# Column sums from the combined weight blocks T4 and T3 of a Strassen-Winograd kernel, with three sums of weight blocks made by accumulating transfers

## The reference

```
h = gelu(cond @ W0 + b0);  h = gelu(h @ W1 + b1)
att = softmax(h @ W2 + b2)                        # 128 samples x 8 kernels
agg_w = sum_k att[b,k] * weight[k]                # one 64x64 channel mix per sample
agg_b = att @ bias_k                              # one bias per sample and channel
y = agg_w[b] @ x[b] + agg_b[b][:, None]           # 128 x 64 x 1024
logits = y @ W_router.T;  top 2 of 8 experts, softmax weights
h = y @ A.T (8 experts x rank 16), weighted by expert
out = x + y @ W_base.T + b_base + (h weighted) @ B * 2.0
```

## Time and profile before

| | us |
|---|---|
| median of 3 runs | 951.85 (951.58 to 951.88) |
| profiled execution, its own time | 951.36 |
| its span, first to last instruction | 949.7 |
| TensorE busy | 942.1 |
| VectorE busy | 786.1 |
| ScalarE busy | 330.0 |
| GpSimd busy | 87.7 |

### The profile page before, as it was taken

The page is one execution under the profiler, slowest core; times in us unless marked ns, Lnnn a source line. Parts: engine busy times, 40 slices in busy tenths (PEclk is TensorE's granted clock), DMA queues, the critical chain, the costliest instruction groups (busy, mean ns, idle before and its releaser), DMA issues.

```text
span 949.7 us, 19258 instructions
## 1 busy us (share of the span) xinstructions
PE 942.1 (99%) x6716; PEld 935.7 (99%) x6716; DVE 786.1 (83%) x2018; ACT 330.0 (35%) x671; POOL 87.7 (9%) x134
## 2 busy tenths in 40 slices
PE   9999999999999999999999999999999999999998
PEld 8999999999999999999999999999999999999997
DVE  4999888888888888888888888888888888888886
ACT  6553332333332333333333333333332333323331
POOL 0011010101010100100000101010101010101010
PEclk9999999999999999999999999999999999999999
DMA  8443444343435344434344434344444444443434
GB/s 303 143 112 96 110 119 132 92 133 91 112 113 134 91 119 107 112 113 125 100 108 119 112 113 111 114 97 129 107 119 104 121 91 121 114 125 99 126 91 111
DMA packets 35234, 111.34 MB, mean 117 GB/s; under 512 B 13040, under 2 KB 13424, under 8 KB 30864
## 3 DMA queue, kind: packets, MB, share of 16 engines
q1 hardware_dynamic: 25712, 76.36, 22.1%
q0 software_dynamic: 9216, 33.56, 21.3%
q10 hardware_dynamic: 288, 1.19, 0.4%
HBM read 75.37 MB, written 35.65 MB: 117 GB/s over the span
## 4 chain that ended last, share of the span: by engine, by line
PE 95%; DVE 2%; DMA 1%; issue 1%; ACT 0%; DVEq 0%; ACTq 0%
PE ps L420 25%; PE ps L424 24%; PE ps L422 24%; PE ps L480 9%; PE ps L456 3%; PE ps L454 3%; PE ps L458 3%; DMA w_stage<-in_wide 1%; PE ps L503 1%; PE ps L446 0%; PE ps L447 0%; DVE x_sb L1025 0%; DMA result<-x_sb 0%; DVE lower_hwT L1007 0%; PE ps L506 0%
## 5 line engine op out<-in xcount | busy, mean ns | idle before, releaser
L420 PE MATMUL ps<-w_hi,x_hi 128*128 128x290 f32 x1544 | 461.0, 299 | 0.9 <-DVE z_lo L960 0.6
L422 PE MATMUL ps<-w_lo,x_hi 128*128 128x290 f32 x1544 | 458.4, 297 | 0.0
L424 PE MATMUL ps<-w_hi,x_lo 128*128 128x290 f32 x1544 | 457.5, 296 | 0.0
L420 PEld LDWEIGHTS ps<-w_hi,x_hi 128*128 128x128 f32 x1544 | 292.4, 189 | 3.5 <-issue 2.6
L424 PEld LDWEIGHTS ps<-w_hi,x_lo 128*128 128x128 f32 x1544 | 291.8, 189 | 0.0
L422 PEld LDWEIGHTS ps<-w_lo,x_hi 128*128 128x128 f32 x1544 | 291.7, 189 | 0.0
L689 ACT CAST x_hi<-xT_sb 128x512 fp32r<-128x512 f32 x186 | 115.6, 621 | 188.7 <-DVE xT_sb L943 166.4
L927 DVE TENSOR_TENSOR x_lo<-xT_sb,x_hi 128x512 fp32r<-128x512 f32 x186 | 127.1, 684 | 22.7 <-ACT x_hi L689 22.7
L904 POOL DMA_DIRECT2D x_sb<-in_x x64 | 56.3, 880 | 534.1 <-DVE x_sb L1025 534.1
L1007 DVE STREAM_TRANSPOSE lower_hwT<-hw 32x32 f32<-32x32 f32 x464 | 93.9, 202 | 13.6
L711 ACT COPY sum<-ps 128x580 f32<-128x580 f32 x96 | 61.6, 641 | 88.1 <-PE ps L424 88.1
(11 more groups left out here) (126 smaller groups left out, 1135.4 us busy)
## 6 DMA issues: line engine op xcount, KB each, us to landing
x_sb<-in_x POOLq DMA_DIRECT2D x64, 512.0 KB, 5.4
result<-x_sb SPq DMA_DIRECT2D x63, 512.0 KB, 2.8
xT_sb<-in_xT SPq DMA_DIRECT2D x31, 1024.0 KB, 4.8
b_sb<-in_wide SPq DMA_DIRECT2D x2, 1160.0 KB, 14.4
agg_w_rows<-agg_w SPq DMA_DIRECT2D x1, 2048.0 KB, 7.5
mix<-agg_w_rows SPq DMA_DIRECT2D x124, 16.0 KB, 3.1
w_stage<-in_wide ACTq DMA_DIRECT2D x2, 580.0 KB, 7.4
w_stage<-in_wide SPq DMA_DIRECT2D x2, 580.0 KB, 10.9
```

Source lines behind the costliest of these rows:

```text
L420: nc.tensor.matmul(dst, x_hi[:, s, rows], high[:, c, cols], start=first, stop=False, skip_group_check=True)
L422: nc.tensor.matmul(dst, x_hi[:, s, rows], low[:, c, cols], start=False, stop=False, skip_group_check=True)
L424: mm = nc.tensor.matmul(dst, x_lo[:, s, rows], high[:, c, cols], start=False, stop=last, skip_group_check=True)
```

## The change

The T's get other signs and another way of being made. T3 is now B12 + B22, T4 is (B21 + B11) - T3, T1 = B12 - B11 as before, T2 = B22 + T1. The signs of S1, S2 and S3 follow. B21 + B11, T3 and T2 are made in place, in the stages of B21, B12 and B22, by accumulating transfers that GpSimd issues in halves (`add_block`): the first two read B11 and the next two B22 from DRAM again, the last two read T1 from the on-chip stage. VectorE makes T1 (now ahead of B22's low part) and T4 only. The column sums run over T4 and T3 in place of B11, B21, B12 and B22: those over T3 are the right half, and those over T4 and T3 together, added on VectorE, the left half. The products A21xB12 and A22xB22 come ahead of the column sums. The small result for agg_b goes to another bank, and ScalarE copies it out instead of VectorE. The low parts of T4, T3 and T2 are all made before unit 1, that of T1 within it, and tile 1's biases come later in unit 1.

```diff
--- before.py
+++ after.py
...
-B11, B21, T1, B22, T2, T4, T3 = range(7)
-B12 = T4
+
+B11, B21, T3, B22, T2, T4, T1 = range(7)
+B12 = T3
...
-        SPLIT_AT = {"B11": 4, "B21": 6, "B12": 7, "B22": 8, "T1": 9, "T2": 10, "T3": 11, "T4": 12}
+        SPLIT_AT = {"B11": 4, "B21": 6, "B12": 7, "B22": 8, "T4": 9, "T3": 10, "T2": 11, "T1": 12}
...
-        T_AT = {"T1": 1, "T2": 2, "T4": 3, "T3": 4}
+        T_AT = {"T1": 1, "T4": 2}
...
-        b11_stage = t_stage = chunked(w_stage[:, 0, :])
+
+        b11_stage = t1_stage = chunked(w_stage[:, 0, :])
         b2_stage = t4_stage = chunked(w_stage[:, 1, :])
-        b12_stage = chunked(b12_sb[:])
-        b22_stage = chunked(b22_sb[:])
+        b12_stage = t3_stage = chunked(b12_sb[:])
+        b22_stage = t2_stage = chunked(b22_sb[:])
...
-            def column_sums(bank, w, start=False, stop=False):
+            def column_sums(bank, w):
                 high, low = weight_parts(w)
                 for part in range(2):
                     dst, cols = ps[:, bank + part, 0:PART], slice(part * PART, (part + 1) * PART)
                     for c in range(CHUNKS):
-                        nc.tensor.matmul(dst, ones_r[:], high[:, c, cols], start=start and c == 0, stop=False)
-                        mm = nc.tensor.matmul(dst, ones_r[:], low[:, c, cols], start=False,
-                                              stop=stop and c == CHUNKS - 1)
-                if stop:
-                    mm.then_inc(col_mm, 1)
+                        nc.tensor.matmul(dst, ones_r[:], high[:, c, cols], start=c == 0, stop=False)
+                        mm = nc.tensor.matmul(dst, ones_r[:], low[:, c, cols], start=False, stop=c == CHUNKS - 1)
+                mm.then_inc(col_mm, 1)
 
...
@@ -568,29 +572,31 @@
             pe.wait_ge(w_lo_done, SPLIT_AT["B22"])
             first_product(b, "A12", B22, False)
             pe.wait_ge(agg_done, 2 * GROUPS)
-            chain(ps[:, O_BANK, 0:BATCH], mix_w_sb[0:KERNELS, GROUP_COLS:MIX_COLS], attT[0:KERNELS, :], agg_b_mm)
+            chain(ps[:, O_BANK + 3, 0:BATCH], mix_w_sb[0:KERNELS, GROUP_COLS:MIX_COLS], attT[0:KERNELS, :], agg_b_mm)
+            first_product(O_BANK, "A21", B12, True)
+            first_product(O_BANK, "A22", B22, False)
             pe.wait_ge(ones_done, 1)
-            column_sums(O_BANK + 2, B11, start=True)
-            column_sums(O_BANK + 2, B21, stop=True)
             pe.wait_ge(agg_b_done, 2)
-            first_product(O_BANK, "A21", B12, True)
-            pe.wait_ge(col_sum_done, 1)
-            column_sums(O_BANK + 2, B12, start=True)
-            first_product(O_BANK, "A22", B22, False)
-            column_sums(O_BANK + 2, B22, stop=True)
+            pe.wait_ge(w_lo_done, SPLIT_AT["T4"])
+            column_sums(O_BANK + 2, T4)
+            pe.wait_ge(z12_summed, 1)
+            pe.wait_ge(w_lo_done, SPLIT_AT["T3"])
+            column_sums(b, T3)
             pe.wait_ge(z22_summed, 1)
             pe.wait_ge(mix_lo_done, 1)
             pe.wait_ge(z11_lo_done, 1)
             mixed(0, 0).then_inc(ar_mm, 1)
             pe.wait_ge(z12_lo_done, 1)
             mixed(0, 1)
-            pe.wait_ge(col_sum_done, 2)
+            pe.wait_ge(col_sum_done, 1)
             mixed(0, 2).then_inc(mixed_mm, 1)
 
             def unit(u, par, first=False):
                 a, b = accumulators(par)
                 pe.wait_ge(z12_summed, u)
                 pe.wait_ge(x_lo_done, splits(u, "A11"))
+                if first:
+                    pe.wait_ge(col_sum_done, 2)
                 product(a, "A11", True)
...
+                if first:
+                    pe.wait_ge(w_lo_done, SPLIT_AT["T1"])
                 product(b, "S1", True)
...
-                if first:
-                    pe.wait_ge(w_lo_done, SPLIT_AT["T3"])
...
-                if first:
-                    pe.wait_ge(w_lo_done, SPLIT_AT["T4"])
...
-            def column_sum(half):
+            def column_sum(half, bank):
                 act.wait_ge(col_mm, half + 1)
                 cols = col_sum[:, half * HALF:(half + 1) * HALF].rearrange("p (k n) -> p k n", k=2)
-                nc.scalar.copy(cols, acc(O_BANK + 2)).then_inc(col_sum_done, 1)
+                nc.scalar.copy(cols, acc(bank)).then_inc(col_sum_done, 1)
...
@@ -787,23 +791,31 @@
             split_weight(B22, b22_stage)
             aggregated(0)
             z11_high(0)
+            act.wait_ge(xT_in, 16)
+            act.wait_ge(product_mm, FIRST_PRODUCT["A11", B12])
+            x_high("A11")
             aggregated(1)
-            act.wait_ge(t_made, T_AT["T1"])
-            split_weight(T1, t_stage)
             act.wait_ge(product_mm, FIRST_PRODUCT["A12", B22])
             save(sum2, b, z12_summed)
-            act.wait_ge(xT_in, 16)
-            x_high("A11")
-            column_sum(0)
+            act.wait_ge(agg_b_mm, 1)
+            for par in range(PAIR):
+                rows = slice(par * CH, (par + 1) * CH)
+                of_tiles = ps[rows, O_BANK + 3, 0:BATCH].rearrange("p (t par) -> p t par", par=PAIR)[:, :, par]
+                nc.scalar.copy(agg_b[rows, :], of_tiles).then_inc(agg_b_done, 1)
+            z12_high(0)
+            x_high("A12")
+            act.wait_ge(t_made, T_AT["T4"])
+            split_weight(T4, t4_stage)
+            act.wait_ge(product_mm, FIRST_PRODUCT["A21", B12])
+            split_weight(T3, t3_stage)
+            act.wait_ge(product_mm, FIRST_PRODUCT["A22", B22])
+            save(sum3, O_BANK, z22_summed)
             for side in range(2):
                 mix_high(0, side)
-            z12_high(0)
-            act.wait_ge(t_made, T_AT["T2"])
-            split_weight(T2, t_stage)
-            x_high("A12")
-            act.wait_ge(product_mm, FIRST_PRODUCT["A22", B22])
-            save(sum3, O_BANK, z22_summed)
-            column_sum(1)
+            act.wait_ge(t2_in, 32)
+            split_weight(T2, t2_stage)
+            column_sum(0, O_BANK + 2)
+            column_sum(1, b)
             act.wait_ge(bT_in, 16)
             nc.scalar.copy(b_hi[:], bT_stage).then_inc(b_hi_done, 1)
...
-                    act.wait_ge(t_made, T_AT["T3"])
-                    split_weight(T3, t_stage)
+                    act.wait_ge(w_lo_done, SPLIT_AT["T3"])
+                    split_weight(T1, t1_stage)
...
-                if first:
-                    split_weight(T4, t4_stage)
...
+            def add_block(dst, block, done):
+                for js in HALVES:
+                    cols = slice(js.start * HALF, js.stop * HALF)
+                    pool.dma_start(dst[:, cols], block[:, cols], accum_op=ALU.add).then_inc(done, 16)
+
+
+            pool.wait_ge(b22_in, 16)
+            pool.wait_ge(w_lo_done, SPLIT_AT["B21"])
+            add_block(w_stage[:, 1, :], wide_blocks[0], left_in)
+            pool.wait_ge(t_made, T_AT["T1"])
+            pool.wait_ge(w_lo_done, SPLIT_AT["B12"])
+            add_block(b12_sb[:], wide_blocks[3], t3_in)
+            pool.wait_ge(w_lo_done, SPLIT_AT["B22"])
+            add_block(b22_sb[:], w_stage[:, 0, :], t2_in)
...
             def make_s1(u):
-                nc.vector.tensor_tensor(raw("S1"), raw("A21"), raw("A22"), ALU.add).then_inc(s_made, 1)
+                nc.vector.tensor_tensor(raw("S1"), raw("A21"), raw("A22"), ALU.subtract).then_inc(s_made, 1)
...
-                nc.vector.tensor_tensor(raw("S3"), raw("A11"), raw("A21"), ALU.subtract).then_inc(s_made, 1)
+                nc.vector.tensor_tensor(raw("S3"), raw("A21"), raw("A11"), ALU.subtract).then_inc(s_made, 1)
...
-                nc.vector.tensor_tensor(raw("S2"), raw("S1"), raw("A11"), ALU.subtract).then_inc(s_made, 1)
+                nc.vector.tensor_tensor(raw("S2"), raw("A11"), raw("S1"), ALU.subtract).then_inc(s_made, 1)
...
             split_weight(B12, SPLIT_AT["B12"], b12_stage)
+            dve.wait_ge(w_lo_done, SPLIT_AT["B11"])
+            make_t(t1_stage, b12_stage, b11_stage)
             split_weight(B22, SPLIT_AT["B22"], b22_stage)
-            dve.wait_ge(w_lo_done, SPLIT_AT["B11"])
-            make_t(t_stage, b12_stage, b11_stage)
             z11_low(0)
             dve.wait_ge(xT_in, 16)
             make_s1(1)
             make_s3(1)
-            dve.wait_ge(agg_b_mm, 1)
-            for par in range(PAIR):
-                rows = slice(par * CH, (par + 1) * CH)
-                of_tiles = ps[rows, O_BANK, 0:BATCH].rearrange("p (t par) -> p t par", par=PAIR)[:, :, par]
-                nc.vector.tensor_copy(agg_b[rows, :], of_tiles).then_inc(agg_b_done, 1)
-            split_weight(T1, SPLIT_AT["T1"], t_stage)
             x_low(1, "A11")
-            dve.wait_ge(w_lo_done, SPLIT_AT["T1"])
-            dve.wait_ge(t_made, T_AT["T1"])
-            make_t(t_stage, b22_stage, t_stage)
+            dve.wait_ge(left_in, 32)
+            dve.wait_ge(t3_in, 32)
+            make_t(t4_stage, t4_stage, t3_stage)
             z12_low(0)
-            dve.wait_ge(t_made, T_AT["T2"])
-            make_t(t4_stage, b2_stage, t_stage)
```

(43 more changed lines are left out.)

## The result

The changed kernel takes 959.85 us (median of 6 runs, 959.19 to 960.6), the kernel before on the same chip 951.87 (951.5 to 952.32): a ratio of 1.0084 [1.0073, 1.0095], 8.0 us slower. The forecast was 956.5, slower with 0.82, with 953 to 959.5 for its main case and 951.8 to 961.5 for 8 in 10: the time lies 0.35 above the first and inside the second. The profiled execution took 960.6 with a span of 958.6, 8.9 over the span of before. The profile first, in the order in which the prediction asked for it.

The account below looks back on a forecast made before the run. The prediction took TensorE to bound the kernel, busy 942.1 of 949.7 us. Unit 1 4.9 later, +0.5 for late bT, -0.3 for unit 2's wait: +5.1 on 951.36 gives 956.5 us, range 951.8 to 961.5 for 8 in 10.

Parts of the forecast that it names:

- T: The moment the first four accumulating transfers have landed, so that VectorE can make T4; taken as 39.0 us.
- What bounds, and the 4.3 us of sums: TensorE bounds the kernel; before unit 1, 32 column-sum matmuls instead of 64 save 4.3 us if nothing it needs comes later.
- faster rival: Accumulating transfers run like plain ones, 1.6 us each, T about 31, unit 1 at 45.2: 946.8 us; chance 0.08.
- T = 39.0, by the mean's price: GpSimd's queue: first landing at 28.3, three more at 3.6 us each, the run's mean for adds of x scaled to 580 KB.
- the pair's price: 3.15 us per further 580 KB transfer, scaled from two adds of x issued one behind the other; would give T 37.8.
- All are queued long before their turn.: GpSimd's issues take 0.9 us each, so all six transfers are queued early and the queue's throughput sets T.
- T2 is needed at T+21.: T2's transfers land by T+7.2, its low part is ready about T+12.4 and needed at T+21.
- T to unit 1, 13.6 + 1.8: From T through T4's parts, the sums and mixing to unit 1: 13.6 us, plus 1.8 for TensorE's slow clock.
- slow stretch: TensorE's column sums and mixing at half clock after about 7 us idle: 0 to 5.9 us, taken as 1.8.
- Late bT, 0 to 1.4, taken 0.5: bT's load waits for agg_w's slowed copy, delaying b_hi and z21 in unit 1: 0 to 1.4 us, taken 0.5.
- the wait of unit 2, -0.3: TensorE's 0.6 us wait early in unit 2 may go as VectorE is 2.5 us lighter: 0 to 0.6, taken 0.3.
- later rival: The fourth transfer shares the engines with agg_w's copy, T = 44.8, unit 1 at 60.2, +10.4: 961.8 us; chance 0.10.

Follow-up runs that it names:

- e4_plain: The changed kernel with its six transfers as plain copies, without accumulation (the additions left out): 947.51 us, 0.9972 of the kernel before.
- e2: The changed kernel with descriptor room for GpSimd's transfers of 3072 instead of 1024: 957.99 us, 1.0072 of the kernel before.
- e3: e2 with 46 thrown-away matmuls while TensorE waits for T4's low part: 959.72 us, 1.0090 of the kernel before.
- g3: f1 with 28 thrown-away matmuls while TensorE waits for T4's low part: 952.42 us, 1.0008 of the kernel before.
- f3: f2 with T3's sums first, B12 sharing its place with T2, and VectorE's work reordered for it: 955.27 us, 1.0035 of the kernel before.
- e1: The changed kernel with ScalarE's first column-sum copy ahead of T2's high part and VectorE's T2 low part behind S2's: 960.04 us, 1.0110 of the kernel before.
- g1: f3 without T2's two transfers; VectorE adds T2 behind T4, ScalarE copies both column sums behind T2's high part: 952.02 us, 1.0004 of the kernel before.
- g2: g1 with T2's low part made inside unit 1 instead of ahead of tile 0's biases: 950.50 us, 0.9991 of the kernel before.
- f4: The changed kernel, unaltered, run again on another chip: 959.62 us, 1.0080 of the kernel before.
- f2: The changed kernel with T3 made by VectorE, leaving four transfers (B21+B11 and T2): 956.06 us, 1.0040 of the kernel before.
- f1: The changed kernel with no accumulating transfers; VectorE makes T3, T2 and T4 = B21 - T2: 953.41 us, 1.0014 of the kernel before.

## Why the prediction was right, and where its sizes were off

The sign, the place and the cause held: four accumulating transfers set T, T sets T4, and TensorE waits in front of the sums. The prediction did not have the second stall, T2's, and it was this one that ended last before unit 1. The time fell in the range for 8 in 10, 3.4 us over the number and just above the 953 to 959.5 that the prediction gave to T from 37 to 42, although T was 40.0: what came behind T was priced too low. By its own steps:

- **What bounds, and the 4.3 us of sums.** Right: 32 matmuls fewer, all credited against waits. The faster rival was nearly right for its condition, which was not met: it said 4.6 us less than before, and e4_plain took 3.3 less than the kernel before on its chip, with landings 1.7 us apart for 1.6, but T at 33.1 for 31 and unit 1 at 46.86 for 45.2.
- **T = 39.0, by the mean's price.** Measured 40.0, and 39.0 in e2. That e2 met the number is luck in part: the first landing was 0.7 late (29.0 for 28.3), and the next three came 3.3 apart, between the pair's price and the mean's. In the changed kernel the fourth was issued at 32.18 in place of 27.4 and met agg_w's copy, issued at 34.08 in place of 38.62; which of the two made T one us later is not separated by any run.
- **"All are queued long before their turn."** This step failed. At most three were out at a time, the sixth was issued at 40.17, and T2's low part was done at 57.8, not at T+12.4 = 51.4. e2 shows that it is GpSimd's descriptor room. With the room given, agg_w's copy and bT were late in T2's place, and the time was the same within the intervals.
- **"T2 is needed at T+21."** Also wrong. Its product needs it then, but ScalarE's copies of the column sums and VectorE's biases and z21 stand behind it in their queues, and need it at once: the biases of tile 0 ended 3.5 us into unit 1 and not 1.1. I traced the moved step's own user and not what is queued behind its wait. Only the chain of waits showed it.
- **T to unit 1, 13.6 + 1.8.** Measured 16.4 against 15.4. The slow stretch came as said, and e3 and g3 price it at 1.3, not 1.8. In the changed kernel the slow stretch was hidden: the sums ended at 54.0, and the third piece of the mixing then had to wait until 55.79 for ScalarE's copy of the column sums, which stood behind T2. So unit 1's start was set by T2, and the 16.4 is T2's time and not T4's. In e2, where T4 set it, it came 15.0 after T.
- **Late bT, 0 to 1.4, taken 0.5; the wait of unit 2, -0.3.** Unit 1 lost 1.8 us over its old length (86.96 - 56.43 = 30.5 against 28.7), 1.0 of it in front of the second product, by T2's queue and not by bT: in the changed kernel b_hi came behind T2 anyway. The mechanism was real all the same (e2, f3), and agg_w's copy ended at 50.2, near the late end of the 42 to 52 that I had given. The 0.6 us wait of before stands at 111.17, in unit 3 (from 107.16) and not in unit 2; in the changed kernel it is gone, and from unit 2's start to the end of the first mixing in unit 3 it took 1.3 us less. The later units and the end took that back (0.8 and 0.7, the last behind the last matmuls), for which the traces show no cause.
- **The sum.** +6.9 for unit 1's start (4.9 said), +1.8 within it (0.5 said), +0.2 later (-0.3 said): +8.9 on the span, +8.0 on the medians. Of the 3.8 us by which the span missed the forecast, 1.0 is T, 2.3 what stands behind T2 and the rest of unit 1, and 0.5 the later units. That T2 carries all of those 2.3 is argued from the chain and from e1, where the two waits behind T2 went and another one came; no run took T2's lateness away without letting bT's in.

The forecast of 956.5 against 959.85 is thus a mis-sized term, the cost behind T, in a right mechanism. The later rival (961.8) had the right idea of sharing with agg_w's copy but the wrong victim: T was held up by one us at most, T2 and agg_w by far more. Its +10.4 leaves out the 0.5 for bT that the forecast counts.

## What to carry to other kernels

An accumulating transfer spares the engine an addition but here delayed whatever shared its queue and the 16 DMA engines: use it early and in the shadow of nothing urgent (g1 and g2 keep two), and not for the operand on which the next step waits. When a step is moved, ask what stands behind its new wait on every engine, not only who uses its result. Taking one stall away showed the next one in most runs here (T4, T2, bT, VectorE in unit 1), so a saving on the bounding engine should be priced only with all the later arrivals in a row.

## What the runs showed of the hardware

- The first four 580 KB accumulating transfers on GpSimd's queue landed 3.6 us apart in the mean in the changed kernel; all six in e2, none held back, 3.8 apart. The same six without accumulation had all landed by about 36, 13 us after the first issue; the accumulating ones took until 53.05, and until about 48 in e2.
- With a descriptor room of 1024 GpSimd had at most three 580 KB accumulating transfers outstanding and was held for 4.8 and 6.2 us before the fourth and the sixth, until the second and the fourth had landed; between 35.2 and 39.9 only two were out. e1 and f4 show the same (4.8 and 6.8). With 3072 all six were out by 30.8 without a hold. Of the plain ones four were out at 27.0 with 1024, and none was held; why they need less room is open.
- A 2 MB copy from SyncE's queue beside them took 16.1 us in place of 7.5, and in e2 its issue came 4.3 us late. One accumulating transfer beside it suffered as much (some 15.7 us in f2, where the one ahead of it took 6.5). The Trainium skill (DMA: Bandwidth & Descriptors, Issuing engines are not separate DMA queues) says that all engines' DMAs run on the same 16 DMA engines and interleave; the trace agrees.
- The granted clock stood at 0.50 after waits of 7.8 us (changed), 4.2 (f1), and 2.9, 2.1 and 1.9 in front of the second product (e3, e2, g1); in e2 and g1 it fell only when matmuls had been running again for about 1 us. Over the 2.1 us in front of the experts in e1 it stayed at 1.00. In the changed kernel the matmuls then ran 0.24 us apart. Keeping TensorE busy through the wait was worth 1.3 us at unit 1's start (e3 beside e2, g3 beside f1).
